# Attention with 16 heads: two pairs of heads scored together, and their V products together

## The reference

```python
Q = (x @ Wq.T + bq).reshape(B, N, H, HD)
K = (x @ Wk.T + bk).reshape(B, N, H, HD)
V = (x @ Wv.T + bv).reshape(B, N, H, HD)
scores = jnp.einsum('bnhd,bmhd->bhnm', Q, K)
scores = scores * (SCALE * adaptive_scale)[None, :, None, None] / TEMP
w = jax.nn.softmax(scores, axis=-1)
attn = jnp.einsum('bhnm,bmhd->bnhd', w, V).reshape(B, N, H * HD)
y = x + (attn @ Wo.T + bo)
return (y - mu) / jnp.sqrt(var + EPS) * gamma + beta
```

## Time and profile before

| | us |
|---|---|
| median of 3 runs | 2625.88 |
| their range | 2622.5 to 2627.6 |
| the profiled execution | 2630.59 |
| its span | 2628.7 |
| PE busy | 2271.8 (86%) |
| ACT busy | 1562.8 (59%) |
| DVE busy | 1547.5 (59%) |
| POOL busy | 1324.9 (50%) |

### The profile page before, as it was taken

One profiled execution on the slowest core, in us unless ns is written; L12 is line 12 of the kernel. 1 busy time (PEld: TensorE's weight loads), 2 busy tenths in 40 slices (PEclk: granted clock), 3 DMA queues, 4 the chain that ended last, 5 costly groups with the idle time before them and its releaser, 6 DMA issues. The chain is left out here.

```text
span 2628.7 us, 52174 instructions
## 1 busy us (share of the span) xinstructions
PE 2271.8 (86%) x17672; PEld 1613.1 (61%) x17672; DVE 1547.5 (59%) x4261; ACT 1562.8 (59%) x3796; POOL 1324.9 (50%) x2132
## 2 busy tenths in 40 slices
PE   6999999999385799998579967999699699997893
PEld 3666666666285466665369954666355367775792
DVE  3576766766621799999653326787300166655375
ACT  3666666666243699999345533787522247774362
POOL 2454545545253788884143236774100268862756
PEclk9999999999787699999779978999899899998995
DMA  4000000000321322220311214442000133311342
GB/s 167 1 1 1 1 1 1 1 1 1 106 65 54 98 65 81 72 65 25 114 53 50 46 46 122 116 114 84 9 0 0 37 110 103 99 55 45 100 144 78
DMA packets 106499, 153.36 MB, mean 58 GB/s; under 512 B 17330, under 2 KB 78660, under 8 KB 99204
## 3 DMA queue, kind: packets, MB, share of 16 engines
q1 hardware_dynamic: 93956, 127.24, 15.5%
q0 software_dynamic: 12288, 22.86, 3.5%
HBM read 100.87 MB, written 47.19 MB: 56 GB/s over the span
## 5 line engine op out<-in xcount | busy, mean ns | idle before, releaser
L181 POOL TENSOR_SCALAR A_prob<-A_prob,A_rinv 128x256 f32<-128x256 f32 x512 | 236.0, 480 | 342.8 <-DVE A_rinv L397 342.7
L993 DVE TENSOR_REDUCE A_nmax<-A_S 128x2 f32<-128x512 f32 (+1 forms) x512 | 311.5, 621 | 144.7 <-PE A_S L770 83.5
L922 ACT ACTIVATE A_PT<-A_E 128x512 f32<-128x512 f32 (+1 forms) x512 | 272.6, 550 | 121.3 <-PE A_E L788 63.2
L349 ACT ACTIVATE A_prob<-A_S,A_nmax 128x256 f32<-128x256 f32 x512 | 235.3, 478 | 4.6 <-DVE A_nmax L392 4.6
L392 DVE TENSOR_REDUCE A_nmax<-A_S 128x2 f32<-128x512 f32 x256 | 164.9, 686 | 93.6 <-PE A_S L268 93.6
L1867 POOL DMA_INDIRECT L_xe<-rows,L_index x112 | 106.5, 951 | 201.8 <-PE L_k L1958 88.3
L1590 DVE TENSOR_SCALAR_CACHE_REDUCE A_D<-A_S 128x256 f32<-128x256 f32 x512 | 193.7, 418 | 14.2 <-PE A_S L1373 13.9
L1596 DVE COPY A_PT<-A_T 128x512 f32<-128x512 f32 x256 | 175.2, 687 | 19.2 <-PE A_T L1386 18.8
L1386 PE MATMUL A_T<-ident_sb,A_D 128*128 128x128 f32 x1024 | 161.4, 281 | 27.2 <-ACT A_D L1515 14.6
L2013 PE MATMUL L_k<-L_w,L_hT 128*128 (+1 forms) x1216 | 167.2, 275 | 0.4 <-ACT L_hT L2159 0.3
L362 ACT ACTIVATE A_OT<-A_O,A_bv 128x256 f32<-128x256 f32 x128 | 60.7, 474 | 178.8 <-PE A_O L295 178.8
(11 more groups left out here) (413 smaller groups left out, 5995.0 us busy)
## 6 DMA issues: line engine op xcount, KB each, us to landing
A_QS<-stack_q SPq DMA_DIRECT2D x144, 192.0 KB
A_KS<-stack_k SPq DMA_DIRECT2D x144, 192.0 KB
results<-L_ye SPq DMA_DIRECT2D x48, 256.0 KB
stack_q<-A_parts SPq DMA_DIRECT2D x48, 192.0 KB
stack_k<-A_parts SPq DMA_DIRECT2D x48, 192.0 KB
L_w<-f_w SPq DMA_DIRECT2D x24, 256.0 KB, 6.7
sent<-A_zeros SPq DMA_DIRECT2D x10, 512.0 KB
L_xe<-sent SPq DMA_DIRECT2D x20, 256.0 KB
```

Of the source, the lines that this page charges most:

```text
L181: nc.gpsimd.tensor_scalar(prob[:, n % NP, j, t, :], prob[:, n % NP, j, t, :], rinv[:, n % NP, j, t:t + 1], 1.0, ALU.mult, ALU.mult).then_i ...
L349: nc.scalar.activation(prob[:, n % NP, j, t, :], psS[n % 2][j][:, t, :], ACT.Exp, bias=nmax[:, n % NP, j, t:t + 1], scale=1.0, accum_out=r ...
L922: nc.scalar.activation(PT[:, n % RING, :], psE[n % 2][:, 0:BLOCKS, :].rearrange("p a b -> p (a b)"), ACT.Exp, scale=scale).then_inc(expd, 1)
L993: nc.vector.tensor_reduce(nmax[:, b % 2, :, h], view, AX.X, ALU.max, negate=True).then_inc(maxed, 1)
```

## The change

PE's scores of two pairs stand together in the even slot, and its V products of two pairs together in the odd slot. The V products of pair n move from slot n+3 to slot n+5 (n even) or n+4 (n odd), into the two halves of psO; `take_o` of both to the even slot after. `exps` and `normalise` of a pair go to the slot of that pair; `exps` stands behind `take_v` now. DVE does four `row_max` in the even slot and none in the odd, and both `invert` in the odd slot, one at its beginning and one at its end. prob and PT have four buffers. V, x and y, `turn` and `project_qk` stay in their slots.

```diff
-    NQ, NP, NT_ = 4, 3, 3
+    NQ, NP, NT_ = 4, 4, 4
...
-    LAG_E, LAG_T, LAG_PV, LAG_O = 1, 2, 3, 4
+    LAG_T, LAG_PV, LAG_O = 2, 5, 6
...
+        def two(s, lag=0):
+
+            return [n for n in (s - lag, s - lag + 1) if s % 2 == lag % 2 and 0 <= n < SLOTS]
...
-                    if (n := pair(slot, LAG_E)) is not None:
+                    if (n := pair(slot)) is not None:
                         normalise(n)
...
-                    after(pe, o_ready, n)
+                    after(pe, o_ready, n - n % 2)
...
-                            i = nc.tensor.matmul(psO[HD * j:HD * (j + 1), 0, :], V[:, b % 2, m, h * HD:(h + 1) * HD], PT[:, n % NT_, j, m, :],
+                            i = nc.tensor.matmul(psO[HD * j:HD * (j + 1), n % 2, :], V[:, b % 2, m, h * HD:(h + 1) * HD], PT[:, n % NT_, j, m, :],
...
-                    if (n := pair(slot)) is not None:
-                        score(n)
+                    if slot % 2 == 0:
+                        for n in two(slot):
+                            score(n)
...
-                    if (n := pair(slot, LAG_PV)) is not None:
-                        weigh(n)
+                    if slot % 2 == 1:
+                        for n in two(slot, LAG_PV):
+                            weigh(n)
...
-                    act.wait_ge(weighed, n + 1)
+                    act.wait_ge(weighed, n - n % 2 + 2)
...
-                    if (n := pair(slot, LAG_O)) is not None:
-                        take_o(n)
-                    if (n := pair(slot, LAG_E)) is not None:
-                        exps(n)
+                    if slot % 2 == 0:
+                        for n in two(slot, LAG_O):
+                            take_o(n)
                     if (n := v_unit(slot)) is not None:
                         take_v(n)
+                    if (n := pair(slot)) is not None:
+                        exps(n)
...
-                    if (n := pair(slot)) is not None:
-                        row_max(n, 0)
-                        row_max(n, 1)
-                    if (n := pair(slot, LAG_E)) is not None:
+                    if slot % 2 == 0:
+                        for n in two(slot):
+                            row_max(n, 0)
+                            row_max(n, 1)
+                    if slot % 2 == 1 and (n := pair(slot, 1)) is not None:
                         invert(n)
...
+                    if slot % 2 == 1 and (n := pair(slot)) is not None:
+                        invert(n)
```

More of the change, by code:

```diff
@@ L358, in take_o @@
                     b, g = divmod(n, U)
-                    act.wait_ge(weighed, n + 1)
+                    act.wait_ge(weighed, n - n % 2 + 2)
                     if g == 0:
                         after(act, y_psum, TB * (b - 1))
-                    nc.scalar.activation(OT[:, b % 2, g, :], psO[:, 0, :], ACT.Identity, bias=bv[:, g:g + 1]).then_inc(o_ready, 1)
+                    nc.scalar.activation(OT[:, b % 2, g, :], psO[:, n % 2, :], ACT.Identity, bias=bv[:, g:g + 1]).then_inc(o_ready, 1)
                 for slot in range(FIRST, LAST + 1):
-                    if (n := pair(slot, LAG_O)) is not None:
-                        take_o(n)
-                    if (n := pair(slot, LAG_E)) is not None:
-                        exps(n)
+                    if slot % 2 == 0:
+                        for n in two(slot, LAG_O):
+                            take_o(n)
                     if (n := v_unit(slot)) is not None:
                         take_v(n)
+                    if (n := pair(slot)) is not None:
+                        exps(n)
                     if (b := at(slot, X_AT)) is not None:
```

## The result

| | us |
|---|---|
| before, median of 4 runs | 2626.74 |
| after, median of 4 runs | 2684.72 (2683.24 to 2687.3) |
| after, profiled execution and its span | 2685.04, 2683.3 |
| ratio | 1.0228, interval 1.0214 to 1.0242 |

A forecast was written before the change was run, and what follows sets the result against it. PE was taken to set the pace of attention 0, busy 198.4 of 200 us. Terms 25 + 9 + 16 + 4 - 2 = +52 us, put on the median 2625.88, gave 2678 us; eight in ten 2648 to 2704.

The forecast's parts named there:

- part 1: Grouping on PE, attention 0: seams saved, 0.46 us for two slots, 64 times, 29.5 us.
- the walk through the plain group: Modelled times of PE, DVE, ACT and POOL over two slots without X or P: 9.40 us where there were 9.00.
- part 2: V directly behind QK waits for take_qk's copy, 1.80 us against 0.86; group +0.40, 63 times, +25 us.
- part 3: X groups: QK waits 1.11 us for take_xT, which stands behind exps; +0.58, 15 times, 9 us.
- part 4: First P slot of a batch: late write_x delays row_max and take_y, so QK waits; 1.1, 14 times, 16 us.
- part 5: inner_norm on DVE, even slot, between row_max and take_qk, delays take_qk: +0.3, 14 times, 4 us.
- part 6: End of attention 0, S of slot 126 to the last batch's first take_y: 19.3 becomes 17 to 18, -2 us.
- rival C: More waits pile up behind the P group, or PE partly gets the lower clock: +24 or more, 2702 to 2710; 10%.
- the base term: Plain groups in attention 0, V's wait against saved seams: +25 us, allowed to go from 20 to 32.
- Rival A: Not slower: seams on PE are saved and V's wait is hidden, 2626 - 30 = 2596; 4%.
- Rival B: Only V's wait counts; X, write_x and inner_norm fit in beside: +25 - 2, so 2649; 12%.

The follow-up runs named there:

- the run without grouping: Kernel before, no grouping, with V put directly behind the QK of the even slot: 2798.14 us, ratio 1.0213.
- the fourth version: Changed kernel with V products ahead of V, write_x behind take_y, take_xT ahead of exps, outer_stats behind take_qk: 2594.47 us, ratio 0.9877.

## Why the prediction was right, point by point

- The seams (part 1): forecast 0.21 for S S, 0.15 for O O, 0.10 for QK; measured 2.13 - 1.93 = 0.20, 2.02 - 1.88 = 0.14. The 0.10 of QK is not seen by itself, since V waits there. The 0.46 left out one thing: T behind V takes 0.88 from start to start (0.93 in the kernel before), and the walk through the plain group had it so without saying it. That is most of why the prediction's 0.94 and 0.46 make 0.48 a group and its walk 0.40; the sum used the walk. With the V products between QK and V the seam from QK to O is back, so 0.36 were to be saved there, and T's 0.05: measured 9.00 - 8.57 = 0.43.
- V's wait (part 2): forecast 1.80 from QK to V, measured 1.81 (364.95 to 366.76 in the run with write_x moved, where nothing else stands in the way). Its cost is the difference between 9.42 and 8.57, 0.85, net of the 0.10 that QK pays in the latter for going over to O, and it stands alone in the run without grouping, 1.04 more there, about 0.1 of it seams. The plain group was forecast at 9.40 and is 9.42: 63 x 0.42 = 26 us. This is shown from both sides, by taking it from the changed kernel and by giving it to the kernel before.
- X groups (part 3): forecast 10.83 with the wait, measured 10.89; +9.4 us. Shown by the move of take_xT (10.34), which also showed that outer_stats stand close behind. In the one such group with no x to turn, slots 2 and 3 of the last batch, the changed kernel already waits for them: V 1.70 us, the group 10.34 in place of 9.42. The prediction put outer_stats at nothing.

```profile
701.74 0.49 DVE L419 BATCH_NORM_STATS2 A_stats<-A_s 128x6 f32<-128x128 f32 x2 [0.57 <-POOL A_s L208]
...
702.36 0.67 DVE L410 TENSOR_TENSOR A_QK<-A_M,A_bqk 128x512 f32<-128x512 f32 x1
...
703.08 1.12 PE L263 MATMUL A_M<-A_wv,A_xT 128*128 128x512 f32 x2 [1.70 <-DVE A_QK L410]
```

- The first P group (part 4): forecast 12.36, measured 12.40 in 13 groups and 12.04 in the first; +15.7 us. Shown by the move of write_x (11.25).
- inner_norm (part 5): forecast +0.3, measured +0.16 (9.58 against 9.42): 2.2 us in place of 4. What DVE needs for the two is 0.51 from start to start (336.83 to 337.34), not 0.6.
- The end (part 6): forecast -2. From S of slot 126 to take_y it is 18.8 in place of 19.3: -0.5.
- Not in the sum: 0.9 us in that group of the last batch, 0.3 in the first two groups (there V waits 1.26 us behind four row_max, but the first S comes 0.4 earlier), and 4.8 us of clock. Three groups of the profiled execution are 1.6 us longer than their like. Timeline of PE in one of them, and its window (columns as in the earlier trace rows):

```profile
167.38 1.13 PE L255 MATMUL A_M<-A_xT,A_wqk 128*128 128x256 f32 x4 [0.99 <-ACT A_xT L341]
...
169.29 2.06 PE L263 MATMUL A_M<-A_wv,A_xT 128*128 128x512 f32 x2 [0.78 <-DVE A_QK L410]
...
171.15 1.82 PE L285 MATMUL A_T<-ident_sb,A_prob 128*128 128x128 f32 x8
```

```profile
163.00:175.70 12.70, 10.93 (x65) 7.29 (x62) 6.60 (x15) 6.93 (x23) 7.07 (x14) 0.87 0.01 1
```

V takes 2.06 in place of 1.12 us and T 1.82 in place of 1.04: from here until the QK at 172.81 PE ran in part at the clock's lower level, 1.2 GHz, behind two waits, of 0.99 and 0.78 us, that stand 1.9 apart. This was in rival C; I had argued from a window with 77% busy in which the clock stayed.

26.5 + 9.4 + 15.7 + 2.2 - 0.5 + 1.2 + 4.8 = 59.3 us, as at the routing line. The forecast was 7 lower for this stage: 4.8 of that were the clock, which the prediction had only in rival C, 1.2 the groups that it left out; the base term and the end were each 1.5 too low, and inner_norm 2 too high. That the medians differ from the forecast by 6 and the profiled executions by 3 is in part chance, since the stages behind took 4.7 us less.
Rival A's time, 2596, was reached by the fourth version (2594), with the seams saved and V's wait hidden by a block between QK and V. That the numbers agree is partly luck: rival A had 0.46 in each of 64 groups, and this version has 0.43, 1.06, 0.31 and 0.43 in the four groups of a batch, the 1.06 with the help of two more moves. Rival B, that the side chains fit in beside, fell with the moves of write_x and take_xT.

## What to carry to other kernels

A block that is moved on a full engine is judged by its new neighbours: list for each shared buffer who writes it next, and lay the copy that frees it (its wait, its length, its place in its own engine's order) against the blocks that are left in between. Grouping blocks of one kind saved 0.43 us a group here, and lost it twice over because the same blocks had been the cover for such a copy; with other cover it gave 1.2%. And when a wait is taken away, look at the next engine in order before adding up: in the X group PE's waits for take_xT and take_qk (0.99 and 0.78 us) had covered that of DVE's outer_stats for POOL, which came out as 1.50 us of PE once they were gone.

## What was not expected of the hardware

The clock fell behind short waits. Three groups of the changed kernel, after PE had been idle twice for 0.8 to 1.0 us, ran V and T at the lower level, 1.6 us lost each time; most groups with the very same waits did not. It happened more often with take_xT moved (six first P groups of 14.0 us, every second one from 214.3 us on, 88.7 us apart) than without (two), though the waits of those groups were alike, and each time behind the wait of 2.64 us (13 groups of 15.06 us), where O O took 3.15 us in place of 1.95. What decides between equal groups is open.

POOL's four multiplications of `normalise` take 1.84 us in one slot of each group of the changed kernel and 2.20 in the other, where DVE's product for the gate has started just before them and runs beside the first. Timeline after, slots 7 and 1:

```profile
332.21 0.68 DVE L457 TENSOR_TENSOR A_gated<-x_state,A_gates 128x512 f32<-128x512 f32 x1
332.39 2.20 POOL L185 TENSOR_SCALAR A_prob<-A_prob,A_rinv 128x256 f32<-128x256 f32 x4 [1.34 <-DVE A_rinv L404]
...
338.81 1.84 POOL L185 TENSOR_SCALAR A_prob<-A_prob,A_rinv 128x256 f32<-128x256 f32 x4 [3.11 <-DVE A_rinv L404]
```

In the kernel before it was in some slots the gate's product that was longer, 1.07 in place of 0.68 us (at 316.17 us), where an addition of POOL had started 0.21 before it; POOL's next addition, beside it, took 1.17 in place of 0.72. That the two engines hold each other up is read from these times alone; no run tests it. Neither was on PE's path.
